# Block 0 of a four-block model: Gelus in one run, operands of VectorE in PSUM, and one product for the division of heads

## The reference, cut to what matters

```python
for i in range(NL):                      # NL = 6, HD = 8
    xn = _adaln(x, noise_emb, n1_w[i], n1_b[i])
    q, k, v = jnp.split(xn @ qkv_w[i].T, 3, axis=-1)
    q, k = _rope(q.reshape(B, L, H, HD)), _rope(k.reshape(B, L, H, HD))
    x = x + _attn(q, k, v.reshape(B, L, H, HD), src_mask).reshape(B, L, D) @ so_w[i].T
    xn = _adaln(x, noise_emb, n2_w[i], n2_b[i])
    q = _rope((xn @ cq_w[i].T).reshape(B, L, H, HD))
    k = _rope((context @ ck_w[i].T).reshape(B, LC, H, HD))
    v = (context @ cv_w[i].T).reshape(B, LC, H, HD)
    x = x + _attn(q, k, v, ctx_mask).reshape(B, L, D) @ co_w[i].T
    xn = _adaln(x, noise_emb, n3_w[i], n3_b[i])
    x = x + (gelu(xn @ f1_w[i].T + f1_b[i]) @ f2_w[i].T + f2_b[i])
# _rope: x1*cos - x2*sin, x1*sin + x2*cos over the two halves of a head
# _attn: softmax(q k / sqrt(HD)) v;  _adaln: layer norm, scaled and shifted
```

## Time and profile before

| | us |
|---|---|
| median of 3 runs | 6271.35 (6262.12 to 6273.82) |
| the profiled execution | 6286.42 |
| its span, first to last instruction | 6284.6 |
| block 0 within the span | about 0 to 3200 |
| PE, DVE, ACT, POOL busy over the span | 5678.5, 3890.6, 3279.5, 2252.9 |
| mean granted TensorE clock | 0.953 |

### The profile page before, as it was taken

The page is one execution under the profiler, slowest core; times in us unless marked ns, Lnnn a source line. Parts: engine busy times, 40 slices in busy tenths (PEclk is TensorE's granted clock), DMA queues, the critical chain, the costliest instruction groups (busy, mean ns, idle before and its releaser), DMA issues.

```text
span 6284.6 us, 140597 instructions
## 1 busy us (share of the span) xinstructions
PE 5678.5 (90%) x55893; PEld 4239.4 (67%) x55893; DVE 3890.6 (62%) x8627; ACT 3279.5 (52%) x6429; POOL 2252.9 (36%) x2204
## 2 busy tenths in 40 slices
PE   5899898988989989889979999999789999989997
PEld 4666666666666666666645777777467777756984
DVE  3877887877878878778854344444544444444553
ACT  1566666656666566566754344444333333333764
POOL 4555655555656555555500000000011111146440
PEclk7999999999999999999988999999899999998998
DMA  2675766767667567576720000000100000021000
GB/s 66 107 117 91 114 108 97 113 99 109 110 96 124 91 106 117 93 109 110 121 55 19 20 30 30 30 30 21 27 16 16 13 14 16 11 91 33 2 2 24
DMA packets 396484, 407.84 MB, mean 65 GB/s; under 512 B 125575, under 2 KB 372946, under 8 KB 393786
## 3 DMA queue, kind: packets, MB, share of 16 engines
q1 hardware_dynamic: 395834, 398.85, 36.3%
HBM read 158.00 MB, written 0.46 MB: 25 GB/s over the span
## 4 chain that ended last, share of the span: by engine, by line
PE 62%; DVE 9%; POOL 9%; issue 7%; SPq 5%; ACT 5%; DMA 3%; POOLq 1%; DVEq 0%; ACTq 0%
PE psum L2273 10%; PE psum L2240 9%; PE psum L1576 5%; PE psum L1562 4%; PE psum L1588 4%; PE psum L2285 4%; PE psum L1610 3%; PE psum L1724 3%; POOL slot_context L3473 3%; SPq L1476 3%; PE psum L1602 2%; PE psum L416 2%; PE psum L430 2%; DVE row_max L1937 2%; SPq L1494 1%
## 5 line engine op out<-in xcount | busy, mean ns | idle before, releaser
L1937 DVE TENSOR_REDUCE row_max<-psum 112x1 f32<-112x500 f32 x2304 | 1442.3, 670 | 234.3 <-PE psum L1576 222.9
L2064 ACT ACTIVATE weights<-psum 125x448 f32<-125x448 f32 x2304 | 1147.3, 541 | 700.4 <-PE psum L1562 687.1
L1576 PE MATMUL psum<-key_stack,query_stack 97*128 97x500 bf16 x2304 | 889.4, 387 | 146.0 <-DVE row_max L1937 70.9
L1562 PEld LDWEIGHTS psum<-query_stack,key_stack 121*128 121x128 bf16 x9216 | 658.7, 100 | 347.9 <-issue 160.9
L1562 PE MATMUL psum<-query_stack,key_stack 121*128 121x112 bf16 x9216 | 849.3, 215 | 7.4 <-ACT weights L2064 2.1
L2353 DVE TENSOR_REDUCE l_stat<-psum 128x1 f32<-128x1500 f32 (+1 forms) x224 | 391.6, 1748 | 546.5 <-PE psum L2240 546.5
L2273 PE MATMUL psum<-l_ctx_v,l_turned 125*128 125x128 f32 x5376 | 713.6, 281 | 16.1 <-ACT l_turned L2311 12.1
L2273 PEld LDWEIGHTS psum<-l_ctx_v,l_turned 125*128 125x128 f32 x5376 | 643.1, 191 | 58.8 <-ACT l_turned L2311 39.9
L1588 PE MATMUL psum<-weights,values 125*17 125x112 f32 x18432 | 562.2, 263 | 0.0
L1588 PEld LDWEIGHTS psum<-weights,values 125*17 125x17 f32 x18432 | 413.9, 98 | 147.6 <-issue 135.1
L2094 POOL TENSOR_TENSOR key_parts<-key_temp,key_parts 128x500 bf16<-128x500 f32 x288 | 327.0, 1135 | 518.9 <-ACT key_parts L1967 518.9
(11 more groups left out here) (539 smaller groups left out, 10421.3 us busy)
## 6 DMA issues: line engine op xcount, KB each, us to landing
key_stack<-key_parts SPq DMA_DIRECT2D x1728, 125.0 KB, 4.6
ctx_t<-in_ctxT SPq DMA_DIRECT2D x96, 750.0 KB
l_ctx_v<-in_ctxV SPq DMA_DIRECT2D x32, 750.0 KB
query_stack<-query_parts SPq DMA_DIRECT2D x576, 28.0 KB, 3.5
l_ctx_t<-in_ctxT SPq DMA_DIRECT2D x16, 750.0 KB
slot_context<-in_ctxV SPq DMA_DIRECT2D x16, 750.0 KB
key_stack<-ctx_mask_rows SPq DMA_DIRECT2D x576, 3.9 KB
sm_w<-in_sm_w SPq DMA_DIRECT2D x3, 2048.0 KB
```

The costliest lines, as they stand in the source:

```text
L1562: mm = e.matmul(self.k.psum[:, h, (p % 4) * QC:(p % 4 + 1) * QC], ks[:, at:at + 128], q[:, p * QC:(p + 1) * QC])
L1576: e.matmul(self.k.psum[:, 2 + n % 2, 0:500], q[0:ROWS_MAX, p * QC:p * QC + 128], ks[0:ROWS_MAX, p, c * 500:(c + 1) * 500]).then_inc(self.m ...
L1937: e.tensor_reduce(self.largest[:, i % PAIRS, i // PAIRS:i // PAIRS + 1], k.psum[0:QC, 2 + i % 2, 0:500], AX.X, ALU.max, negate=True).then_ ...
L2064: e.activation(half(self.p[kt % RING_P], h), self.k.psum[0:KN, h, 0:HALF], ACT.Exp).then_inc(self.exped.sem, 1)
```

## The change

Four edits, all in block 0. (1) All four up products and Gelus of an MLP stand in step 13, with one load of each table set, where there were two and two in steps 13 and 14. (2) The negated maxima lie in the last eight columns of the "rows" bank of PSUM instead of in SBUF, so VectorE waits for that bank first. (3) The rotation's swapped halves and sine product stay in the rotation's PSUM bank instead of SBUF; the order is cosine, shuffle, sine, sum, and the bank is given back at the end, after a drain. (4) The odd turned blocks are written 8 columns further left, so that all 16 heads lie 32 columns apart, and the division is one product of 128 columns instead of four of 32.

```diff
-T_UP, ... = {13: (0, 1), 14: (2, 3)}, ...
+T_UP, ... = {13: (0, 1, 2, 3)}, ...
...
-            if f % 2 == 1:
+            if f == 3:
                 e.preload_act_table_set(LN_EXP)
...
             for i in range(4):
-                tr = e.transpose(side.bank(*key)[0:S, i * 128:(i + 1) * 128], self.acc[:, i * S:(i + 1) * S],
-                                 k.ident[:, :])
+                at = i * 128 - 8 * (i % 2)
+                tr = e.transpose(side.bank(*key)[0:S, at:at + 128], self.acc[:, i * S:(i + 1) * S], k.ident[:, :])
...
     def max_parts_vector(self, e, s):
-        neg, m = self.neg, self.m_part[:, 1:1 + 3 * PAIRS].rearrange("q (p j) -> q p j", j=3)
+        side, key = self.side, ("rows", s)
+        neg, m = side.bank(*key)[0:QC, BANK - PAIRS:BANK], self.m_part[:, 1:1 + 3 * PAIRS].rearrange(
+            "q (p j) -> q p j", j=3)
+        e.wait_ge(side.emptied(*key), side.before(*key))
         e.wait_ge(self.max_read.sem, self.max_read(s, 3 * PAIRS - 1))
...
     def divide(self, e, key, inv, o, inverted, value):
-        e.reciprocal(inv.rearrange("p (m j) -> p m j", m=4),
-                     bk.rearrange("p (m j c) -> p m j c", m=4, j=4)[:, :, :, 0]).then_inc(inverted.sem, 1)
+        sums = bk.rearrange("p (g c) -> p g c", g=2)[:, :, 0:240].rearrange("p g (h c) -> p g h c", h=2)
+        e.reciprocal(inv.rearrange("p (g h j) -> p g h j", g=2, h=2), sums[:, :, :, 0:97:32]).then_inc(inverted.sem, 1)
         e.wait_ge(inverted.sem, value)
-        blocks = bk.rearrange("p (g c) -> p g c", g=2)
-        for g in range(2):
-            for h2 in range(2):
-                v = blocks[:, g, 128 * h2:128 * (h2 + 1)].rearrange("p (j c) -> p j c", j=4)[:, :, 1 + 8 * h2:9 + 8 * h2]
-                m = 2 * g + h2
-                op = e.tensor_tensor(o[:, m * 32:(m + 1) * 32].rearrange("p (j d) -> p j d", j=4), v,
-                                     spread(inv[:, 4 * m:4 * m + 4], 8), ALU.mult)
-        op.then_inc(side.emptied(*key), 1)
+        e.tensor_tensor(o.rearrange("p (m d) -> p m d", d=8), bk.rearrange("p (m c) -> p m c", c=32)[:, :, 1:9],
+                        spread(inv, 8), ALU.mult).then_inc(side.emptied(*key), 1)
...
-            e.stream_shuffle(other, bk, OTHER_HALF).then_inc(self.rope_turned.sem, 1)
             e.scalar_tensor_tensor(out=by_batch(o), in0=by_batch(bk), scalar=scale, in1=cs, op0=ALU.mult,
-                                   op1=ALU.mult).then_inc(side.emptied(*key), 1)
-            e.wait_ge(self.rope_turned.sem, self.rope_turned(ph, n))
-            e.scalar_tensor_tensor(out=by_batch(other), in0=by_batch(other), scalar=scale, in1=sn, op0=ALU.mult,
+                                   op1=ALU.mult).then_inc(self.rope_turned.sem, 1)
+            e.wait_ge(self.rope_turned.sem, self.rope_turned(ph, n, 0))
+            e.stream_shuffle(bk, bk, OTHER_HALF).then_inc(self.rope_turned.sem, 1)
+            e.wait_ge(self.rope_turned.sem, self.rope_turned(ph, n, 1))
+            e.scalar_tensor_tensor(out=by_batch(bk), in0=by_batch(bk), scalar=scale, in1=sn, op0=ALU.mult,
                                    op1=ALU.mult).then_inc(self.rope_sin.sem, 1)
-            e.wait_ge(side.emptied(*key), side.after(*key))
             e.wait_ge(self.rope_sin.sem, self.rope_sin(ph, n))
-            e.tensor_tensor(o, o, other, ALU.add).then_inc(self.roped.sem, 1)
+            e.tensor_tensor(o, bk, o, ALU.add).then_inc(self.roped.sem, 1)
+            e.drain().then_inc(side.emptied(*key), 1)
```

More of the change, by code:

```diff
@@ L1242 @@
 T_NORM = {"mlp": 6, "self": 16, "cross": 64}
-T_UP, T_DOWN, T_ROPE, T_SV = {13: (0, 1), 14: (2, 3)}, 15, {23: 0, 24: 1, 71: 2}, 24
+T_UP, T_DOWN, T_ROPE, T_SV = {13: (0, 1, 2, 3)}, 15, {23: 0, 24: 1, 71: 2}, 24
 QUARTER = HALF // 2
@@ L1295, in __init__ @@
             self.largest = sb("row_max", [QC, PAIRS, 3])
-            self.neg = sb("neg_max", [QC, PAIRS])[:, :]
             self.m_part = sb("neg_max_parts", [QC, WIDE], BF16)[:, :]
@@ L1367, in __init__ @@
         ropes = [(ph, n) for ph in PHASES if NEXT_OF(ph) is not None for n in range(3)]
-        self.rope_turned = Ordered(k, "l0_rope_turned", ropes)
+        self.rope_turned = Ordered(k, "l0_rope_turned", [(*key, i) for key in ropes for i in range(2)])
         self.rope_sin = Ordered(k, "l0_rope_sin", ropes)
@@ L1740, in phase_tensor @@
                 for m in range(4):
-                    tr = e.transpose(side.bank(*key)[0:S, m * 128:(m + 1) * 128], self.sacc[:, m * S:(m + 1) * S],
-                                     k.ident[:, :])
+                    at = m * 128 - 8 * (m % 2)
+                    tr = e.transpose(side.bank(*key)[0:S, at:at + 128], self.sacc[:, m * S:(m + 1) * S], k.ident[:, :])
                 tr.then_inc(side.filled, 1)
@@ L1861, in phase_vector @@
             cs, sn = (a[:, 0:S].unsqueeze(1).broadcast_to([128, BH, S]) for a in (self.cos, self.sin))
-            bk, other = side.bank(*key)[:, 0:HALF], half(k.sq, 1 - c)
+            bk = side.bank(*key)[:, 0:HALF]
             o = half(self.k_rot if n == 1 else self.q_rot, c)
```

## The result

| | before | after |
|---|---|---|
| median, us | 6272.59 (6262.12 to 6280.45) | 6188.85 (6173.94 to 6192.31) |
| span of the profiled execution | 6284.6 | 6190.5 |
| VectorE busy over the span | 3890.6 | 3746.2 |

The ratio is 0.9863, 95% interval [0.9841, 0.9885]. The forecast was 6196.

A forecast was written before the change was run, and what follows sets the result against it. Block 0 was taken as bound by TensorE's work, its waits and the lower clock behind stalls. 21 + 13 + 12 + 25 + 13 - 10 = 74, about 75 us off 6271.35, gave 6196; range 6140 to 6250.

The forecast's parts named there:

- The split: Block 0, t = 34: operands in PSUM end TensorE's 1.95 us wait for the parts, 11 times: 21 us.
- Eaten: At t = 22 and 70 the 1.0 us saved is waited again at L1699 for GpSimd's norm: zero.
- Rival (b): More comes back: GpSimd's norm ends sooner, 1.0 us at t = 22 and 70 kept; 6142 us; chance 0.08.
- The rotation: Block 0, t = 26: chain of k 2.7 us, stall 4.01 to 2.5; net 1.15 us x 11 = 13 us.
- In place in PSUM: Rotation's shuffle and sine product within one PSUM bank cost nothing extra; at most double time, 42 us in all.
- The Gelus: MLP of block 0: no wait for the value copy, down product 1.0 us sooner, x 12 = 12 us.
- The division: Block 0: one product for four gains zero, VectorE being ahead there; without that cover below 0.5 us x 192.
- The clock: Half speed behind stalls: split's 25 us back whole, rotation's 13 of 33, less 10 for longer waits at L1699.
- rival (d): Slower: merged waits at L1699 drop the clock at all 22 places, at worst 5 us each: 6297; chance 0.06.
- signs named for being wrong: New waits on the up products, on the first value product behind n = 0, or on VectorE ahead of the split.
- Rival (a): The clock doesn't come back; falls move to other stalls of 2 us: 6225 to 6235; chance 0.18.
- Rival (c): Operands in PSUM don't end the waiting for GpSimd; only the Gelus count: 6259; chance 0.08.

The follow-up runs named there:

- e2: Kernel before with only the split's operands moved to PSUM; 6231.66 us, ratio 0.9948.
- e1: Kernel before with only the Gelu edit; 6255.3 us, ratio 0.9987.
- e4: Kernel before with only the one-product division; 6267.53 us, ratio 1.0000.
- e7: The changed kernel with the old division of four products and the old transposes; 6184.12 us, ratio 0.9847.
- e6: The changed kernel with both halves of a norm in one GpSimd step; 6170.13 us, ratio 0.9829.
- e6b: The same kernel as e6, timed again; 6163.25 us, ratio 0.9844.
- e5: Kernel before with GpSimd's multiply held back until the rotation of k is over, rotation still in SBUF; 6245.33 us, ratio 0.9965.
- e3: Kernel before with only the rotation in PSUM; 6253.25 us, ratio 0.9983.
- c1: The changed kernel once more, unaltered, beside the kernel before on another chip; 6186.07 us, ratio 0.9856.
- e9: Kernel before with the split and the rotation in PSUM, without the Gelus and the division; 6201.21 us, ratio 0.9892.

## Why the prediction was right

It was right in its place and its mechanism, and the time came out near: 6188.85 measured, 6196 forecast. That the sum is so near is in part luck, since terms that were too small and costs that were left out nearly cancel. By its own steps:

- *The split*, 21 us. Its waits fall by 46 us, those at L1698 rise by 25 (25.7 to 50.8): net 21. "Eaten" is exact, and e2 shows it alone. Rival (b) is out.
- *The rotation*, 13 us. The chain of k takes 2.6 us against 2.7 said (by the 2.7 the sum would have been 1.7 off the stall, not 1.5). The stall is 0.4 to 1.96 us at ten places and none at one, not 2.5, and the row maxima's waits fall by 33 us. The term was too small, because TensorE also comes to the place later, held at L1698: in e2, where the rotation is untouched, they already fall by 15.
- *Small waits*, at nothing. Against the 71 us that these two and the up products' wait for the value copy give, 20 us of small waits come up at other places (the self attention's mask product 6, the exponentials behind the MLP 5, which the Gelu step had named, and some shorter ones). So TensorE waits 52 us less from 200 to the end of the stretch, where the three terms said 46.
- *In place in PSUM*: no cost. Shuffle 628 ns, sine product 632; the upper bound (near 1.2 us) is out. The 65 ns more for each PSUM operand, the prediction's estimate from the Trainium skill ("VectorE: DVE Perf Modes", section on the TRN2 errata), don't show: the 8-column subtraction takes 175 ns from PSUM and 168 from SBUF.
- *The Gelus*, 1.0 us in each phase. From the first up product to the down product it was 8.64 us in nine of eleven phases; in five of after it is 7.7, so 0.94. In two more it is 8.5, and in four the clock falls behind the wait for the up product's norm (one phase in before) and 9.4 are left. e1, timed, gives 8 us against 12.
- *The division*: nothing, by e4 and e7.
- *The clock*, 25 + 13 - 10 = 28 us. The table gives 41 us less at half speed, worth 20.5, so the sum is near and both of its halves are off. No fall stands behind the rotation or the split any more, so 25 and 33 came back, not 25 and 13. But behind the longer waits at L1698 the clock fell at 16 of 22 places, with 64.6 us at half speed in the ten us behind them: 32 us, not 10. This is rival (d)'s mechanism at some 1.5 us a place, under the 3.9 from which it decides. e6 confirms the cause: with these waits at 1.23 us the falls behind them are gone, though in e6b two stand behind the rotation again.

Of the signs named for being wrong none came in any size: two waits of an up product for a Gelu (1.1 us in all), five of the first value product (1.7 us), and VectorE isn't held by the bank ahead of the split.

Rival (a), that the falls move to other stalls, holds for half of them: of the 118 us at half speed behind the two stalls of before, 63 are back behind L1698 in after. Its time, 6225 to 6235, is out. Rival (c) is out by the durations.

## What to carry to other kernels

On a path that one engine's order sets, count waits and lower clock place by place: a stall removed is worth what isn't waited for again at the next stop, and when two short waits merge into one long one, price the clock behind it. An operand moved to PSUM or a neighbour moved away cures the same contention; moving it only pays where TensorE waits for it. After such an edit read the wait list again: here the wait that grew, for a GpSimd row with other work ahead of it, held nearly as much again.

## What the runs showed of the hardware

- VectorE reads and writes one PSUM bank in place at no loss: a shuffle of 128x448 took 628 ns from PSUM to PSUM and 662 from PSUM to SBUF.
- GpSimd is slowed too: its multiply of 128x896 took 2.06 us beside VectorE's sine product and sum of two SBUF inputs and 1.69 where these were moved (after) or over (e5).
- A cast of 8 columns from SBUF, with one input, took 178 to 1277 ns in before; from PSUM 172 to 177 in after.
- Waits of 1.2 us at the rotation's product were seldom followed by half speed in the next ten us (3 of 22 in before, 5 at most, in e3, none in e6b), waits of 2.3 us mostly (15 to 19 of 22 in e2, after, e7, c1 and e9). Waits of 1.95 us differ by the place and from execution to execution: behind the split 5 to 10 of 11 in six traces, behind the rotation none of four in after, 3 of 8 in e6 and 5 of 8 in e3. What decides there, the runs don't show.
